# ScalarE makes the high halves of the hidden activations, the block table comes in two parts, and three weights' low parts come one block earlier

## The reference, cut to what matters

```python
scores = jnp.einsum('bnd,ed->bne', x, expert_tokens)
_, topk_idx = jax.lax.top_k(scores, TOP_K)
for i in range(num_expert):
    w = jnp.mean((topk_idx == i).astype(x.dtype), axis=-1, keepdims=True)
    h = jax.nn.gelu(jnp.einsum('bnd,dh->bnh', x, W1[i]) + b1[i], approximate=False)
    h = jax.nn.gelu(jnp.einsum('bnh,hk->bnk', h, W2[i]) + b2[i], approximate=False)
    y = jnp.einsum('bnh,hd->bnd', h, W3[i]) + b3[i]
    outputs = outputs + y * w
```

## Time and profile before

| | |
|---|---|
| median of 3 runs | 381.18 us (379.96 to 381.94) |
| the profiled execution's own time | 380.43 us |
| its span, first to last instruction | 378.7 us |
| mean granted clock of TensorE | 0.918 |
| PE busy | 295.6 us (78%) |
| PEld busy | 180.4 us (48%) |
| DVE busy | 275.8 us (73%) |
| ACT busy | 185.2 us (49%) |
| POOL busy | 155.7 us (41%) |

### The profile page before, as it was taken

The page is one execution under the profiler, slowest core; times in us unless marked ns, Lnnn a source line. Parts: engine busy times, 40 slices in busy tenths (PEclk is TensorE's granted clock), DMA queues, the critical chain, the costliest instruction groups (busy, mean ns, idle before and its releaser), DMA issues.

```text
span 378.7 us, 7685 instructions
## 1 busy us (share of the span) xinstructions
PE 295.6 (78%) x2441; PEld 180.4 (48%) x2441; DVE 275.8 (73%) x722; ACT 185.2 (49%) x410; POOL 155.7 (41%) x239
## 2 busy tenths in 40 slices
PE   3957688889897875377976899999987848999910
PEld 2543333333433423164644566666654844687710
DVE  3788769988997564985778488888888689747603
ACT  7650726657675453433624255555553224476602
POOL 8303164645563248763254222332222000577860
PEclk9966989999999999779889899999999988899975
DMA  5589478974530005525247511211000310111114
GB/s 158 200 206 261 162 225 280 246 274 132 159 112 4 1 2 155 184 86 167 78 137 228 145 30 29 64 50 30 23 16 16 111 57 1 34 37 44 50 49 166
DMA packets 21029, 41.75 MB, mean 110 GB/s; under 512 B 3294, under 2 KB 11710, under 8 KB 20992
## 3 DMA queue, kind: packets, MB, share of 16 engines
q0 software_dynamic: 8288, 27.05, 22.7%
q1 hardware_dynamic: 11998, 12.85, 12.5%
q10 hardware_dynamic: 706, 1.38, 1.1%
HBM read 26.59 MB, written 14.43 MB: 108 GB/s over the span
## 4 chain that ended last, share of the span: by engine, by line
PE 33%; DVE 27%; DMA 11%; POOL 11%; issue 10%; ACT 6%; SPq 1%; ACTq 1%; DVEq 0%; POOLq 0%
PE pair L1197 9%; POOL y_rows L790 5%; DVE mA L1569 4%; DMA w_ring<-in_L_ffn_W_dram 3%; PE bank L1094 3%; DVE w_sb L1506 3%; PE bank L1207 3%; PE pair L1185 2%; ACT h L883 2%; PE bank L1218 2%; PE bank L1086 2%; POOL x_slots L718 2%; DVE z L1696 2%; PE pair L1050 2%; POOL tg L779 2%
## 5 line engine op out<-in xcount | busy, mean ns | idle before, releaser
L1197 PE MATMUL pair<-w_sb,h 128*128 (+1 forms) x276 | 66.7, 393 | 3.9 <-DVE w_sb L1506 2.9
L692 POOL TENSOR_SCALAR_AFFINE_SELECT p_ring<-p_ring 128x128 f32<-128x128 f32 (+2 forms) x88 | 38.7, 464 | 58.4 <-ACT p_ring L872 57.8
L872 ACT ACTIVATE p_ring<-bank 128x512 f32<-128x512 f32 (+1 forms) x88 | 44.9, 566 | 32.3 <-PE bank L1073 31.9
L1569 DVE TENSOR_REDUCE mA<-pair 128x2 f32<-128x256 f32 (+3 forms) x64 | 50.4, 817 | 13.2 <-PE pair L1052 13.0
L883 ACT ACTIVATE h<-pair,cols 128x128 f32<-128x128 f32 x92 | 26.2, 368 | 55.9 <-PE pair L1185 54.6
L768 POOL DMA_INDIRECT y_rows<-y_sb,id_now x19 | 23.2, 1223 | 70.6 <-DVE y_sb L1727 66.0
L1197 PEld LDWEIGHTS pair<-w_sb,h 128*128 128x128 f16 x276 | 26.5, 101 | 34.7 <-issue 4.9
L1050 PE MATMUL pair<-kr,qr 128*128 128x128 bf16 (+3 forms) x128 | 34.8, 329 | 6.8 <-DVE mA L1569 5.4
L847 ACT ACTIVATE w_sb<-w_ring 128x1024 f16<-128x1024 f32 x24 | 25.4, 1058 | 29.2 <-DMA w_ring<-in_L_ffn_W_dram 29.2
L883 ACT ACTIVATE h<-bank,cols 128x128 f32<-128x128 f32 x92 | 26.5, 387 | 11.2 <-PE bank L1207 11.1
L1073 PE MATMUL bank<-qr,kr 128*128 128x512 bf16 (+3 forms) x128 | 29.8, 302 | 1.5 <-ACT p_ring L872 1.1
(11 more groups left out here) (313 smaller groups left out, 606.7 us busy)
## 6 DMA issues: line engine op xcount, KB each, us to landing
w_ring<-in_L_ffn_W_dram POOLq DMA_DIRECT2D x24, 512.0 KB, 5.1
x_slots<-w_sb POOLq DMA_DIRECT2D x4, 1032.0 KB, 8.4
fc_sb<-in_L_ffn_c_fc_dram POOLq DMA_DIRECT2D x4, 512.0 KB, 4.1
cp_sb<-in_L_ffn_c_proj_dram POOLq DMA_DIRECT2D x4, 512.0 KB, 5.6
back<-y_rows SPq DMA_DIRECT2D x8, 256.0 KB, 3.3
kr<-k_rows SPq DMA_DIRECT2D x8, 204.0 KB
qr<-q_rows SPq DMA_DIRECT2D x8, 192.0 KB
xg<-x_slots SPq DMA_DIRECT2D x20, 64.5 KB, 2.1
```

The source lines that it names most:

```text
L692: pool.affine_select(out=probs, in_=probs, compare_op=ALU.is_ge, fill=0.0, base=0, pattern=[[0, heads], [1, P]], channel_multiplier=-1).th ...
L872: act.activation(p_ring[:, w % P_RING, 0:width], bank(4 + v % 3)[:, 0:width], ACT.Exp).then_inc(exp_done, 1)
L1197: ins = mm(bank(3), h1[:, s, hq, k * P:(k + 1) * P], w2_sb[k][wq][:, bass.ds(e * HID, HID)], start=(k == 0 and n == 0), stop=(k == HC - 1 ...
L1569: dve.tensor_reduce(mA[:, b, t, g * G + 2 * hp:g * G + 2 * hp + 2], got[:, :, 0:(t + 1) * P], AX_X, ALU.max).then_inc(a_used, 1)
```

## The change

Three edits, all in the stage of the first mixture. ACT gets two functions that make the high halves of h1 and h2 with a Copy that scales by IN_UP; DVE's `split_1` and `split_2` keep only the low half, and wait for ACT's. In DVE's loop the result of block i-1 is put ahead of `split_1(i + 2)`. The three low parts move from blocks 3 to 5 to blocks 2 to 4, ahead of the table, and the table is made in two halves, the first in block 2, the second in block 3.

```diff
@@ ACT @@
+            def hidden_high_1(i):
+
+                s = i % 2
+                act.wait_ge(gelu1_done, i + 1)
+                if i >= 2:
+                    act.wait_ge(mm2_done, i - 1)
+                act.activation(h1[:, s, 0, :], h32[:, 0], ACT.Copy, scale=IN_UP).then_inc(hi1_ready, 1)
+
+            def hidden_high_2(i):
+
+                s = i % 2
+                act.wait_ge(gelu2_done, i + 1)
+                if i >= 2:
+                    act.wait_ge(mm3_done, i - 1)
+                act.activation(h2[:, s, 0, :], h32[:, 1], ACT.Copy, scale=IN_UP).then_inc(hi2_ready, 1)
...
             gelu1(0, 0)
+            hidden_high_1(0)
             gelu1(1, 1)
+            hidden_high_1(1)
             of = list(range(LEAD))
             for i in range(NB):
                 if i == 1:
                     gelu2(1, of[1])
+                    hidden_high_2(1)
                 if i + 2 < NB:
                     gelu1(i + 2, of[i + 2])
...
                 if i != 1:
                     gelu2(i, of[i])
+                if i + 2 < NB:
+                    hidden_high_1(i + 2)
+                if i != 1:
+                    hidden_high_2(i)
                 if SPLIT_AT <= i < SPLIT_AT + 2 * E:
                     high_weights(i - SPLIT_AT)
@@ DVE @@
-            def block_table():
-
+            def block_table(half):
+
+                if half:
+                    rows_of_blocks()
+                    return
...
                 step(dve.tensor_reduce(tabf[:, 1, :], endblk[:, :, :], AX_X, ALU.add))
 
+            def rows_of_blocks():
+
                 step(tt(tabf[:, 2, :], bidx[:, :, 0], tabf[:, 1, :], ALU.subtract))
...
-                ts(h1[:, s, 0, :], h32[:, 0], IN_UP, None, ALU.mult).then_inc(hi1_ready, 1)
                 dve.wait_ge(hi1_ready, i + 1)
...
-                ts(h2[:, s, 0, :], h32[:, 1], IN_UP, None, ALU.mult).then_inc(hi2_ready, 1)
                 dve.wait_ge(hi2_ready, i + 1)
...
                     copy_x(i + 3)
+                if i:
+                    result(i - 1, of[i - 1])
                 if i + 2 < NB:
                     split_1(i + 2)
-                if i:
-                    result(i - 1, of[i - 1])
                 split_2(i)
-                if i == 2:
-                    block_table()
-                if i >= 3 and i - 2 + LAST_PAIR < W_TILES:
-                    low_part(i - 2 + LAST_PAIR)
+                if i >= 2 and i - 1 + LAST_PAIR < W_TILES:
+                    low_part(i - 1 + LAST_PAIR)
+                if 2 <= i < 4:
+                    block_table(i - 2)
```

## The result

The changed kernel takes 388.25 us (median of 4 runs, 387.31 to 389.52) against 380.57 for the kernel before beside it (4 runs, 379.37 to 381.94): a ratio of 1.0203, with a 95% interval of 1.0154 to 1.0251. That is 7.7 us slower; 5.8 were forecast. Some executions show a lower granted clock and a longer time: the ratios and their intervals leave them out, so a ratio is not always the quotient of the two medians. The profiled execution took 389.52 us and has a span of 387.8.

A forecast was written before the change was run, and what follows sets the result against it. A loop of waits over PE, ACT and DVE was taken as the bound, 4.88 us per block. Terms +2.3 (blocks 0 to 7), +2.5 (to block 20), +1.0 (end) gave +5.8: 380.43 to 386.2 us, range 381.9 to 389.0.

The forecast's parts named there:

- High halves to ACT: Blocks 7 to 20: ACT's high 1 stands behind gelu2, tail grows to 4.54, 0.19 per block, 2.5 us slower.
- The result costs nothing: DVE's loop: the result (0.26 us), moved ahead of low 1 into the wait for ACT, adds no time.
- The last blocks: Blocks 20 and 21: loop closes over one block, high 2 on ACT costs more; 1.0 us slower together.
- Entry: Blocks 0 to 3: first rows' load covers blocks 0 and 1; z of block 3 comes 0.5 us later.
- The table's second half: End of block 3: table ready late, block 7's rows land after 5.1; net +2.3 us over blocks 0 to 7.
- quick copy: ACT's high-half Copy takes 0.60 us instead of 0.68; tail growth 0.15 per block instead of 0.19.
- Quick rows: Rival: block 7's rows land in 1.7 to 3.6 us, total only +2.4 to +4.3, 382.8 to 384.7; chance 0.15.
- Harmless order: Rival: ACT's order does no harm, period stays 4.88, only the table's term is left, 380.4 to 382.7; chance 0.10.
- faster: Rival: DVE's relief counts in full, PE bounds the blocks, period about 4.68, 373.4 or 376.4 us; chance 0.10.

The follow-up runs named there:

- e8: Kernel before with the table in block 1, low parts in blocks 2 to 4, low weights one block later ahead of `split_1`: 370.73 us, ratio 0.9809.
- e11: Second run, for a narrower interval, of the kernel before with early table, earlier low parts and later low weights: 370.86 us, ratio 0.9751.

## Why the prediction was right, and where it missed

Slower was right, and both mechanisms were there; the amount was 5.8 forecast, 6.3 in the blocks of the traces and 7.7 in the medians. The interval of the ratio reaches from 5.9 to 9.6 us, so the blocks' 6.3 lies in it, and what makes up the rest of the 7.7 stays open. That the sum came so near is in part luck: the period's term was too small and the table's term too large. Step by step:

- **High halves to ACT.** Forecast 2.5 us from block 7 to 20, measured 3.5 (67.37 less 63.85). The term was mis-sized at two places. The wait from ACT's Copy to DVE is 0.14 us (267.91 to 268.05), not the 0.03 that stands between gelu and L1704 in the earlier trace rows. And I had taken the loop over two blocks, with its tail of 4.54, as the one that sets the period; the one over a single block, which I wrote down only for the last blocks, is as long with the old 0.03 (0.74 + 0.66 + 0.14 + 1.00 + 0.68 + 0.03 + 0.61 + 0.61 + 0.60 = 5.07, for 5.07 over two) and longer with 0.14. The operation itself was 0.65 us (629 to 679 ns), between the two rows I had. The rule of the Trainium skill (ScalarE: Activation LUTs, What ACT_TABLE_LOAD costs), 186 ns and 0.833 ns per element, gives an estimate of 0.61 for it, a little under the measured one; its overlap of 93 ns with the neighbour is near the 0.12 seen here (0.64 long, the next 0.52 later).
- **"The result costs nothing."** True in the changed kernel, and wrong as the reason was put: it did not move into a free wait, it got a wait of its own of 1.16 for the third layer. That it is harmless depends on ACT being later still. The run with the swap alone (ratio 1.0232) shows it.
- **The last blocks.** 1.0 forecast, 0.95 measured: 0.69 in block 20 and 0.26 in block 21. The mark of the earlier trace rows is the one of block 20.
- **Entry.** z of block 3 was to come 0.5 later by block 2's longer work; the distance from block 2 to 3 grew by 0.26. That splitting the table removes no wait was right. That the load of the first rows covers blocks 0 and 1 was right too: 17.97 and 17.70 us from gelu1 of block 0 to z of block 2.
- **The table's second half.** Ready 6.92 after z of block 3, forecast 6.95. The landing took 3.9 for 5.1. In return the low clock reached over transposes and third layer too (0.4 + 0.66 on top of 1.36), where I had counted 1.5 for the second layer alone. From z of block 3 to the second layer of block 5 it was 13.94 for the 14.15 forecast (8.47 before): two errors that nearly cancel. The prediction had no word of PE's own wait of 2.73 for the table; it lies ahead of the wait for the rows and adds nothing to it. Between z of blocks 2 and 7 the changed kernel lost 1.8; forecast +2.3 up to block 7's second layer.
- **The range.** Its ends were added up a little too wide. With the rival's own rows the low end is 382.1 and not 381.9 (0.04 x 13 and twice 0.08 are 0.7 for the quick copy), and the high end 388.7 and not 389.0. The measured 388.25 lies inside either way, near the top.
- **Rivals.** Quick rows: the landing of 3.9 was just above the 1.7 to 3.6 assigned to it, and the sum went the forecast's way. The rival drew on the rule that the DMA engines go round the queues packet by packet (the Trainium skill, DMA: Bandwidth & Descriptors, Queues, rings and completion order). The rows here don't look like it: the small load landed 0.2 us behind the large one sent 2.1 us ahead of it (206.94 and 206.75). It was 0.1 before (205.0 and 204.87) and 0.2 with the loads later (202.95 and 202.73). In the run with the early table four such loads, sent 1.0 to 2.1 us behind a cp_sb load, all landed 0.1 to 0.3 behind it. What holds the small load, the queues or the memory, was not tried. Harmless order and faster: both fall with the period of 5.14. For the faster one I wrote that high 1 would have to start at 1.2, which it can if gelu2 is not in front of it. In the run with high 1 first it did start at 1.17, and the period was 5.18: low 2 then waits for high 2.

## What to carry to other kernels

In a pipeline over several engines, ask of each edit which loops of waits run through the engine's queue order and how many blocks they span. DVE had 19 us less work and the kernel was slower; a swap of two calls that adds no work cost 2.3%. What pays is taking work out of the stretch between the last arrival and the first thing that the next block needs: 0.6 us of independent work moved into an existing wait brought the period from 5.14 to 4.81, near the 4.80 where PE is nearly always busy. A table that several engines read belongs in an idle stretch soon after its input is known, with its first reader's transfer counted in, but behind what another engine waits for in that stretch. And a yardstick that begins behind the place where a repair puts its work hides what the repair costs.

## What was not expected of the hardware

- DVE starts 0.14 us after the end of ACT's Copy on 128x512 (267.91 to 268.05; 0.10 to 0.14 in all runs that have it), and 0.03 after the recorded end of a gelu group.
- A stand of 3.2 us for a load, behind one of 2.7 for the table, left TensorE at a granted clock of 0.58 for 207 to 213, most of it at 1.2 GHz. The layer in it took 4.11 us for 2.75. In the run with the table alone it took 4.56. The length of a stand alone doesn't tell whether the clock falls: behind the 2.67 us for z at 196.16 it was 1.00 (196.1 to 197.6), behind the 2.38 us in the kernel before (192.77) it was 0.64 (192.7 to 195).
- A load of block rows (64.5 KB) with nothing beside it took 1.7 to 2.1 us to land. Behind a load of 512 KB in flight, sent 2.1 us ahead, it landed 0.2 us after that one (206.94 and 206.75).
- The stretch ahead of the blocks varies by itself: the same kernel run twice (e8 and e11) has its first z at 173.80 and 176.49, while blocks 2 to 22 take 96.84 and 97.29. Medians of few runs carry this; the distances within the blocks do not. What makes it vary wasn't tried.
